# Two routed-linear stages of a one-core transformer stack: gathers in order of token tile, mixing and turning at other places, a sixth PSUM bank in the down phases, expert numbers loaded into registers in twos

## The reference, cut to what matters

```
def _L2_ffn_ref(x, router_gate, w_gate, router_up, w_up, router_down, w_down):
    def _moe_linear(x, router_w, expert_w):   # top 2 of 8 experts
        vals, idx = jax.lax.top_k(x @ router_w.T, 2)
        probs = jax.nn.softmax(vals, axis=-1)
        ...
        for e in range(8):
            out = out + combine[:, e:e + 1] * (x @ expert_w[e].T)
        return out
    g = _moe_linear(xt, router_gate, w_gate)      # 128 -> 512
    u = _moe_linear(xt, router_up, w_up)          # 128 -> 512
    inter = jax.nn.silu(g) * u
    return _moe_linear(inter, router_down, w_down) # 512 -> 128
```

## Time and profile before

| | us |
|---|---|
| median of 3 runs (2835.11 to 2844.81) | 2844.01 |
| the profiled execution, device time | 2840.57 |
| its span in the trace | 2838.8 |
| PE busy over the span | 2446.1 (86%) |
| DVE / ACT / POOL busy | 1644.3 / 1458.5 / 782.3 |
| mean granted TensorE clock | 0.932 of 2.4 GHz |
| stage A, first to last matmul | 345.8, PE busy 280.5 |
| stage B, first to last matmul | 352.0, PE busy 284.0 |

### The profile page before, as it was taken

The page is one execution under the profiler, slowest core; times in us unless marked ns, Lnnn a source line. Parts: engine busy times, 40 slices in busy tenths (PEclk is TensorE's granted clock), DMA queues, the critical chain, the costliest instruction groups (busy, mean ns, idle before and its releaser), DMA issues. The chain is left out here.

```text
span 2838.8 us, 41435 instructions
## 1 busy us (share of the span) xinstructions
PE 2446.1 (86%) x13335; PEld 1250.0 (44%) x13424; DVE 1644.3 (58%) x2954; ACT 1458.5 (51%) x3263; POOL 782.3 (28%) x828
## 2 busy tenths in 40 slices
PE   7989999987886899999999878877788758887888
PEld 3446666654883222222222248743333533433333
DVE  5778888855225888888888512212434522434554
ACT  3662333333653588888887855444433336334344
POOL 1235666621235200000000012343333023343112
PEclk9988999998997799999999989978989979999999
DMA  4353223211672220120100027656544028455112
GB/s 153 93 154 103 89 92 100 85 39 51 180 199 65 52 41 14 22 33 12 31 14 3 3 79 247 201 168 238 184 161 138 1 81 274 167 176 160 27 42 65
DMA packets 205399, 286.50 MB, mean 101 GB/s; under 512 B 24688, under 2 KB 128624, under 8 KB 202448
## 3 DMA queue, kind: packets, MB, share of 16 engines
q1 hardware_dynamic: 186792, 233.94, 27.5%
q0 software_dynamic: 18432, 50.36, 5.8%
HBM read 176.17 MB, written 107.73 MB: 100 GB/s over the span
## 5 line engine op out<-in xcount | busy, mean ns | idle before, releaser
L3177 DVE TENSOR_REDUCE big<-psum 128x2 f32<-128x1024 f32 x512 | 603.8, 1221 | 76.6 <-PE psum L2974 72.7
L3131 ACT ACTIVATE probs<-psum 128x512 f32<-128x512 f32 x1024 | 553.5, 600 | 143.7 <-PE psum L2995 128.3
L2995 PE MATMUL psum<-big,k_ops 128*128 128x512 bf16 x944 | 294.3, 386 | 13.4 <-ACT probs L3131 6.9
L1722 PE MATMUL psum<-big,turned 128*128 x480 | 249.7, 644 | 27.5 <-ACT turned L1874 16.9
L1815 PE MATMUL psum<-big,probs 128*128 128x512 f32 x512 | 243.4, 629 | 19.3 <-DVE down_sum L1994 19.3
L2995 PEld LDWEIGHTS psum<-big,k_ops 128*128 128x128 bf16 x1024 | 81.3, 97 | 335.9 <-ACT probs L3131 261.7
L1428 ACT ACTIVATE hidden<-psum,big 128x128 f32<-128x128 f32 x480 | 135.8, 374 | 140.2 <-PE psum L1321 89.1
L1882 ACT ACTIVATE big<-psum 128x512 f32<-128x512 f32 x240 | 141.2, 595 | 124.3 <-PE psum L1722 94.8
L1675 POOL DMA_INDIRECT big<-linear_y,linear_row x128 | 123.4, 964 | 275.8 <-PE psum L1722 179.6
L644 POOL DMA_INDIRECT linear_rows<-desk_tokens,linear_row x128 | 126.0, 984 | 245.9 <-DVE linear_row L620 106.5
L2974 PE MATMUL psum<-big,w_A_or_L_A 32*128 32x512 bf16 x1024 | 163.6, 397 | 27.0 <-DVE big L3177 15.4
(11 more groups left out here) (500 smaller groups left out, 3985.0 us busy)
## 6 DMA issues: line engine op xcount, KB each, us to landing
linear_y<-big SPq DMA_DIRECT2D x240, 256.0 KB
big<-in_experts SPq DMA_DIRECT2D x120, 322.0 KB
big<-step_rows SPq DMA_DIRECT2D x16, 1024.0 KB
qkv_chunks<-big SPq DMA_DIRECT2D x48, 256.0 KB, 2.3
big<-qkv_chunks SPq DMA_DIRECT2D x16, 768.0 KB
big<-linear_rows SPq DMA_DIRECT2D x48, 256.0 KB
big<-since_rows SPq DMA_DIRECT2D x32, 256.0 KB
big<-row_store SPq DMA_DIRECT2D x32, 256.0 KB, 5.0
```

Source lines behind the costliest of these rows:

```text
L1722: pe.matmul(k.bank[bank_of(n, m)][:, :], turned[:, q % 2, t % 4, :], w["up" if r else "gate"][:, bass.ds(experts[r][t] * TB, TB)], start=T ...
L2995: pe.matmul(k.bank[2 + m % 3][:, :], k_ops[:, g % 2, h, kt * P:(kt + 1) * P], q_ops[:, g % 2, i % QB, h, :], start=True, stop=True).then_i ...
L3131: act.activation(probs[:, kt % 2, h, :], k.bank[2 + m % 3][:, :], ACT.Exp, scale=SCALE).then_inc(expd.sem, 1)
L3177: dve.tensor_reduce(into, k.row_pair[hp].rearrange("p (h t) -> p h t", h=2), AX.X, ALU.max).then_inc(row_max.sem, 1)
```

## The change

- The gathers go token tile by token tile: (0,0) (0,1) (1,0) (1,1) ...; the pacing by tile stays.
- `mixing`: j = 0, 1, 2 at m = 10, 18, 26 (in E2 at 14, 20, 27); PE turns five tiles later instead of three, so that j = 2 is turned after the first half of the down phase. In D2 the last block's j = 0, 1 are mixed at q = 2, 5, and j = 2, 3 at q = 0, 1 of D3.
- Down phases use six banks, 2 to 7, by a table; expand tiles start at bank 5 instead of 3.
- Registers are loaded two at a time at every second tile (r = 1 at m = 0 to 14, in E0 also block 1's at m = 15 to 29), and three at a time in the down phase for block n + 2.
- Stage A's leftover gathers come ahead of the scatter of block 2, which is released earlier; its mix moves to q = 2 of D0 and its turn to m = 1 of E2.
- Router, norm and `turn_y` steps move to other tiles. In D3, `turn_y(2)` and DVE's `add_to_x(2)` move from q = 0 and 1 to q = 3.

```
-    BANKS = 5
+    ROUTE_AT, RANK_STEP = (-3, 0, 15, 0), (5, 5, 5, 7)
+    BANKS, DOWN_BANKS, TURN_AFTER = 5, ((2, 3, 4, 5, 6, 7, 3, 4), (2, 5, 6, 7, 3, 4, 2, 5)), 5
...
         def mixing(n):
-            return {12: (n - 1, 0), 17: (n - 1, 1), 25: (n - 1, 2)} if n > 0 else {}
+            at = {0: (), NB - 2: (14, 20, 27)}.get(n, (10, 18, 26))
+            return {m: (n - 1, j) for j, m in enumerate(at)}
...
         def mixing_down(n):
-            last = {3: (NB - 1, 0), 4: (NB - 1, 1), 6: (NB - 1, 2)} if n == NB - 2 else {}
-            return {1: (n, TPB - 1), **last}
+            last = {NB - 2: {2: (NB - 1, 0), 5: (NB - 1, 1)}, NB - 1: {0: (NB - 1, 2)}}
+            return {**last.get(n, {}), 1: (n, TPB - 1)}
+
+        def turning(n):
+            late = [mixing(n + 1)[m] for m in mixing(n + 1) if m + TURN_AFTER >= TILES] if n + 1 < NB else []
+            return {**{q + 1: of for q, of in mixing_down(n).items()}, **{0: of for of in late}}
...
-            return 3 + m % (3 if ahead and n == NB - 1 else BANKS)
+            return 3 + (m + 2) % (3 if ahead and n == NB - 1 else BANKS)
...
-                for j, r in ((0, 0), (1, 0), (0, 1), (1, 1), (2, 0), (2, 1), (3, 0), (3, 1)):
-                    if j < 2:
+                for j, r in ((j, r) for j in range(TPB) for r in range(ROUTERS)):
+                    if j == 0:
...
-                if n + 1 < NB:
-                    scatter(n + 1, lambda step: at_half(n - 1, step // 2 - 1) if step > 1 else None)
                 if left and n == 1:
                     left.gather(pool, TPB, 2 * TPB)
+                    scatter(n + 1, lambda step: at_half(n - 1, step * 3 // 8))
+                elif n + 1 < NB:
+                    scatter(n + 1, lambda step: at_half(n - 1, step // 2 - 1) if step > 1 else None)
...
-                        if m in (3, 7, 11):
-                            load_experts(n, 1, (m - 3) // 4 * 5, (m - 3) // 4 * 5 + 5)
-                        elif m in (20, 24, 28) and n + 1 < NB:
-                            load_experts(n + 1, 0, (m - 20) // 4 * 5, (m - 20) // 4 * 5 + 5)
+                        if m < SLOT_TILES and m % 2 == 0:
+                            load_experts(n, 1, m, min(m + 2, SLOT_TILES))
+                        elif n == 0 and m >= SLOT_TILES and m % 2:
+                            load_experts(1, 0, m - SLOT_TILES, min(m - SLOT_TILES + 2, SLOT_TILES))
...
                         down(n, q)
+                        if n + 2 < NB and q < 5:
+                            load_experts(n + 2, 0, 3 * q, 3 * q + 3)
```

More of the change, by code:

```diff
@@ L1769, in route_block @@
                     route.pe_tokens(pe, n, k.bank[0], xn)
-                elif step == 5:
+                elif step == RANK_STEP[n]:
                     route.pe_rank(pe, n)
             def last_norm(m):
-                if m == 1:
-                    turn_y(0)
-                elif left and m == 3:
+                if left and m == 1:
                     pe.wait_ge(down_route.shifted.sem, down_route.shifted.at(0))
                     left.turn(pe, k.bank[1])
-                elif m == 5:
+                elif m == 6:
+                    turn_y(0)
+                elif m == 8:
                     if left:
@@ L1805, in down @@
                     pe.wait_ge(inter_out.sem, inter_out.at(4 * n + j))
-                if q >= BANKS:
-                    pe.wait_ge(down_used.sem, down_used.at(n * HALVES + q - BANKS))
+                bank = down_bank(n, q)
+                mine = [earlier for earlier in range(q) if down_bank(n, earlier) == bank]
+                if mine:
+                    pe.wait_ge(down_used.sem, down_used.at(n * HALVES + mine[-1]))
                 elif n == NB - 1:
-                    pe.wait_ge(down_used.sem, down_used.at((n - 1) * HALVES + last_half(3 + q)))
+                    pe.wait_ge(down_used.sem, down_used.at((n - 1) * HALVES + last_half(n - 1, bank)))
+                elif bank == 2:
+                    pe.wait_ge(slots_out.sem, slots_out.at(group_of(n + 1, 1, 3)))
                 else:
-                    into = [m for m in range(TILES) if bank_of(n + 1, m) == 3 + q]
+                    into = [m for m in range(TILES) if bank_of(n + 1, m) == bank]
                     if into:
@@ L2003, in prepare @@
                 if n == 2:
-                    if m == 1:
+                    if left and m == 1:
+                        left.add(dve, k.bank[1])
+                    elif m == 6:
                         add_to_x(0)
-                    elif left and m == 2:
-                        left.mix(dve)
-                    elif left and m == 4:
-                        left.add(dve, k.bank[1])
-                    elif m == 7:
+                    elif m == 10:
                         norm.dve_invert(dve, 3)
-                    elif m == 9:
+                    elif m == 13:
                         norm.dve_norm(dve, 3)
-                step = m - (-3 if n == 0 else 11 if n == 2 else 0)
+                step = m - ROUTE_AT[n]
                 if n + 1 < NB:
@@ L2041, in _ @@
                     for m in range(TILES):
-                        prepare(n, m)
-                        if n == 3 and m == 2:
-                            add_to_x(1)
                         if m in mix_at:
@@ L2048, in _ @@
                             multiply(*mix_at[m - 2])
+                        prepare(n, m)
+                        if n == 3 and m == 6:
+                            add_to_x(1)
                         if ahead and n == NB - 1:
@@ L2052, in _ @@
                     for q in range(HALVES):
-                        if n == NB - 1 and q == 1:
-                            add_to_x(n - 1)
+                        if left and n == 0 and q == 2:
+                            left.mix(dve)
                         if q == 3:
                             down_route.dve_weights(dve, n)
+                            if n == NB - 1:
+                                add_to_x(n - 1)
                         if q in mixing_down(n):
```

66 lines of the change are left out of this document (36 added, 30 removed).

## The result

| | before | changed |
|---|---|---|
| median of 4 runs each on one chip | 2840.78 us | 2737.97 us |
| lowest to highest | 2835.11 to 2844.81 | 2734.02 to 2741.07 |
| profiled execution, device time | 2840.57 | 2741.07 |
| mean granted TensorE clock | 0.932 | 0.939 |
| stage A, first matmul to last | 345.8, PE busy 280.5 | 290.7, PE busy 262.5 |

The account below looks back on a forecast made before the run. Bound: PE (86% busy) and its waits in stages A and B, with DMA the next limit in expand phases. Terms: 28 + 9 + 6 + 6 + 3 + 3 + 10 - 8 = 57 us, giving 2787 against the median; range 2756 to 2830.

Parts of the forecast that it names:

- (g): PE in both stages: fewer waits keep the granted clock higher, a fifth of some 55 us, 10 us gained.
- W: Theory for the experiments: each PE wait brings the low clock along, costing itself and about half as much again.
- P: Theory for the experiments: PE's waits cost only themselves, and the rest of the gain came from somewhere else.
- N: Theory for the experiments: gather and turn order is worth little; banks, loads or leftover carries most.
- (h): Expand phases: DMA takes back gain as gathers land later and the store ring fills, -8 us.
- R1: Rival: DMA bounds the expand phases, which can't average more than 278 GB/s; 2803 us, chance 0.17.
- (a): Both stages: PE's waits for the mixed product fall from 48.9 to 21 us, 28 gained.
- R2: Rival: waits only move, ACT standing for gathers at m = 18 and 26, PE behind it; 2822 us, chance 0.14.
- (b): Both stages: PE's waits for slots late behind ACT, 16.8 us in all, 9 gained; E0's end stays.
- (c): Down phases: six banks shorten the first two's waits; the last, ending with DVE, gains nothing; 6 us net.
- (e): Register loads: a load of two costs 0.8 us in traffic, covered by two tiles; 3 us gained.
- R4: Rival, more than forecast: PE holds clock 1.00, (g) 25 and (a) 35 us; 2765 us, chance 0.07.

Follow-up runs that it names:

- E0: Not a run: the first expand phase of a stage, in the kernel before and the changed one alike; no time of its own is given.
- u_gather: Changed kernel with the gathers back in the order (0,0) (1,0) (0,1) (1,1): 2737.76 us, ratio to the kernel before 0.9774.
- u_turn3: Changed kernel with PE turning three tiles behind the mix instead of five: 2731.89 us, ratio to the kernel before 0.9747.
- u_banks5: Changed kernel with five banks in the down phases, expand tiles still starting at bank 5: 2734.99 us, ratio to the kernel before 0.9755.
- u_mix: Changed kernel with old gather order, turns three tiles behind and most mixes at their old places: 2757.83 us, ratio to the kernel before 0.9846.
- u_three: Changed kernel with five banks, expand-phase register loads in fives and the old leftover together: 2774.59 us, ratio to the kernel before 0.9782.
- u_left: Changed kernel with stage A's leftover gathers, mix and turn placed as before: 2743.98 us, ratio to the kernel before 0.9687.
- E3: Not a run: an expand phase of each stage; from before to changed, 44.2 to 34.6 us in stage A and 51.7 to 40.6 in B.
- u_rot5: Changed kernel with five banks in the down phases and the tiles' bank rotation of before: 2715.27 us, ratio to the kernel before 0.9692.
- u_fives: Changed kernel with expand-phase registers loaded in fives, the down phases' threes kept: 2713.35 us, ratio to the kernel before 0.9680.
- c_after: The changed kernel run again, unaltered, in a later set: 2704.68 us, ratio to the kernel before 0.9663.
- woven kernel: Changed kernel with the last block's mixes and turns spread between DVE's down halves; its second run took 2692.83 us against 2704.68 for the changed kernel.
- u_places: Changed kernel with mixes at m = 12, 17, 25 in every expand phase, turned five tiles later: 2742.57 us, ratio to the kernel before 0.9670.
- v_weave: First run of the woven kernel, without the changed kernel beside it: 2732.77 us, ratio to the kernel before 0.9634.
- first and third set: Run groups: u_gather, u_turn3, u_fives, u_banks5; later c_after, u_rot5, u_mix, woven kernel. The kernel before took 2799.7 and 2800.4 us in them.

## Why the prediction was right in direction and wrong in size

**The failed step is (g), the clock.** It put a fifth of the waits' length on top, 10 us; measured were 32.4, half of the 66.0 of standing that went, while the granted clock rose from 0.91 and 0.92 to 0.96 and 0.95 in the two stages. The gap of 22 is half of what the sum missed. Undoing a part shows the same: u_gather 17.6 still and 10.2 busy, u_turn3 16.2 and 7.2, u_banks5 22.7 and 17.0, u_mix 33.4 and 20.6, u_three 20.5 and 16.7. W holds at 0.4 to 0.8 for each of them, each figure uncertain by some 4 us of busy time, and u_left shows it in one place. P falls, since the busy time moves with the same number of matmuls; N falls with u_mix. The rows for it were there, and they disagree: behind a wait of 3.18 3 us were lost in 16 records, and behind one of 3.19 nothing in 24. The text used the second only as the measure of full clock, and chose a fifth because "other waits nearby stay". In the expand phases they did not stay: in E2 of A PE stood still for 15.5 us and stands still for 0.1.

**(h) was wrong: DMA took back little** (-8 forecast; in E1 and E3 of stage A, the two phases of its floors, PE stands still for 1.2 and 2.7 us in all, and waits for slots behind late gathers are among them). The floor of 40.2 us assumed that E1 must carry all of its 14.2 MB. It needn't. D0 of stage A, before and then changed (the E1 ahead of it is in the earlier trace rows and above):

```profile
1971.40:2005.70 34.30, 30.77 (x106) 14.05 (x105) 15.73 (x49) 4.93 (x8) 17.29 (x18) 0.98 0.23 75
```

```profile
1951.27:1987.85 36.58, 32.10 (x111) 14.75 (x109) 19.14 (x52) 7.42 (x13) 21.93 (x22) 0.95 0.41 141
```

Before, 278 x 51.1 and 75 x 34.3 are 14.2 and 2.6 MB; now 335 x 36.0 and 141 x 36.6 are 12.1 and 5.2. E1 carries 2 MB less and D0, where the queues have room, 2.6 more; ACT waits for gathers there (at most 2.2 us), but PE waits for no product. At a DMA share of 0.99 E1 has no room left; R1's limit of 278 GB/s was none.

**(a) product waits**: 28 forecast, 41 measured (48.9 to 8.0). The two waits in D2, 4.4 forecast each, are there. The timeline of the changed kernel's D2 in stage A:

```profile
2124.51 0.66 PE L1746 MATMUL psum<-w_const,big 128*128 128x128 f32 x4 [4.06 <-DVE big L1999]
```

What did not come is the 1 us at each of twelve turns: a break-even was priced as a loss. R2, that the waits only move, is refuted with it: PE's waits for slots did not grow, and ACT's for gathers fell from 43.8 to 27.9.

**(b) slots**: 9 forecast, 3 measured (16.8 to 14.0). The wait at E0's end grew, from 3.2 to 4.8 in stage A. The first record of E1, and one tile later on:

```profile
1915.28 2.07 PE L1734 MATMUL psum<-big,turned 128*128 x2 [4.84 <-ACT turned L1894]
...
1936.22 1.12 PE L1734 MATMUL psum<-big,turned 128*128 x2 [1.21 <-ACT turned L1894]
```

**(c) banks**: 6 forecast, 4.8 measured alone in u_rot5 and 7.7 between the two profiles (bank waits 19.3 to 5.4, the last `turn_y` of each stage 3.6 to 9.8). The wait at q = 6 was put at 1.4, and D3's end at T + 4.9 + 8 x 1.73, whatever the banks. Both are there (1.57, and an end within 0.2 us of that sum):

```profile
2048.35 3.67 PE L1833 MATMUL psum<-big,probs 128*128 128x512 f32 x8 [1.57 <-DVE down_sum L2014]
...
2166.36 0.92 PE L1755 MATMUL psum<-w_const,down_sum 128*128 128x128 f32 x4 [4.73 <-DVE down_sum L2014]
```

**(d) leftover**: 5.8, all of it, right; u_left shows 7.1 of wait and 3 more of clock. **(e) loads**: 3 forecast; PE's waits without cause fell by about 10 (6.4 + 1.9 and 2.0 + 2.4 to 0.8 + 1.5), but u_fives brings back only 2 of standing, so most of these 10 came with the other parts, or with the loads that went to the down phases, which u_fives left there. The price of a load of two was right in traffic (0.8) and too low in quiet (0.3 against 0.53), which did not matter here. **(f) norms**: 3 forecast, 2.9 measured (3.4 to 0.5); another norm wait of stage B, L179 with 4.6 us, went too, 7.5 in all (in c_after 5.7).

**A loss that no term had.** The router turned back (L242) waits 4.8 us in stage A (3.8 in D0, 1.0 in D2) and 5.9 in B (4.6 in c_after); before it waited nowhere. In B's D2 the cause can be seen, first on ACT, then on PE:

```profile
2504.69 0.72 ACT L1906 ACTIVATE big<-big,w_L 128x512 f32<-128x512 f32 x1 [8.44 <-DMA big<-linear_y,linear_row]
```

```profile
2507.08 0.48 PE L242 MATMUL psum<-w_const,down_route_logT 128*128 128x128 f32 x1 [5.91 <-ACT down_route_logT L236]
```

ACT scales the first token tile of the last block at q = 2 now, ahead of the router's logits, and its gather is not there. The prediction followed PE past this point and not ACT. The woven kernel has it after the logits, and its L242 waits 0.4. In stage A's D0 the cause stays open: ACT stands 8.23 us, and the trace shows no releaser of this core:

```profile
1971.47 0.28 ACT L236 ACTIVATE down_route_logT<-psum 128x128 f32<-128x128 f32 x1 [8.23 <-remote]
```

In c_after, the same kernel, it isn't there (its D0 takes 32.8 us, not 36.6), so the change alone doesn't make it. D0 of u_places and v_weave has it as the first profile has (36.8 and 36.6 us, 3.8 and 3.9 at L242), and no profile of the first and third set shows an ACT wait with this releaser. Nothing was tried on it.

The sum with what was measured, in standing time, in the order of the terms (a) to (f) and L242 last: 41 + 3 + 8 + 6 + 10 + 7.5 - 11 = 64 of the 66, and 32 by the clock. Of the rivals R4 was nearest, right in kind (few waits, PEclk 1.00 in E2) and still too small: it had 25 for the clock and 35 for (a), and left (h) at -8.

## What to carry to other kernels

When waits are taken from TensorE, look at the rows behind several such waits (how much longer the next matmuls take than at full clock) and price the waits by these too, without a discount for neighbours which the same change removes. Single waits differ much; here the whole came to half of the standing time. A bound from a phase's bytes holds only for bytes that somebody waits for in that phase, so look whether the next phase's queues are idle before calling it a floor. Where a step is moved ahead of another in one engine's stream, follow each engine past that point, the one that merely copies too, since its wait for a transfer becomes everyone's. And when several parts are undone in one kernel, look at its waits for some that neither the kernel before nor the changed one has: they are a cost of the mixture and belong to no part.

## What the runs showed of the hardware

- **Waits and the clock.** From the woven kernel to the one before, PE's busy time for the same matmuls in the two stages goes from 525.2 to 564.6 us as its standing time goes from 53.6 to 133.3, about half a us for each us; the others lie between. Single waits scatter: 3.1 us lost behind one of 7.06 (u_left), 3.0 behind one of 3.18, 1.8 behind one of 2.90 and 0.1 behind one of 3.19 (both u_rot5).
- **DMA.** 335 and 345 GB/s, at a share of 0.99 and 1.00, held for a whole phase of 36.0 and 35.7 us (E1 of the changed kernel, twice), stores and indirect gathers together; the earlier trace rows had shown 353 for 10 us only.
- **Register loads.** In the changed kernel one register takes 307 ns at least, two 530 (median 803), three 767 (median 924) and fifteen 1572; in u_fives five take 588 (median 1788). So the shortest load of five is shorter than that of three, and the median is 1.5 times the shortest for two registers and 3 times for five.
